# Constant matmuls in TensorE's waits, at the end of a token front and in an attention's lead (Trainium2, one core)

## The reference

```python
h = tok(x)                                  # 36 patches an image: layernorm, 768 -> 256, layernorm, + position
h = concat([cls_tok, h], axis=1)            # 38 tokens an image, width 256
h = h + L0_attn(layernorm(h))               # 16 heads of 16, 4 key/value heads, causal, ternary weights
h = h + L0_ffn(layernorm(h))                # shared expert and one of 8 routed experts
h = h + L1_attn(layernorm(h))               # integer-quantised attention
h = h + L1_ffn(layernorm(h))                # three low-rank-corrected blocks
```

## Time and profile before

| | us |
|---|---|
| median of 3 runs | 531.59 |
| lowest and highest of them | 531.07, 534.79 |
| the profiled execution, its time | 535.75 |
| its span, first to last instruction | 533.9 |
| TensorE busy | 413.0 |
| VectorE busy | 313.8 |
| ScalarE busy | 243.6 |
| GpSimd busy | 154.4 |
| mean granted TensorE clock, as a share of full speed | 0.862 |

### The profile page before, as it was taken

One profiled execution on the slowest core, in us unless ns is written; L12 is line 12 of the kernel. 1 busy time (PEld: TensorE's weight loads), 2 busy tenths in 40 slices (PEclk: granted clock), 3 DMA queues, 4 the chain that ended last, 5 costly groups with the idle time before them and its releaser, 6 DMA issues.

```text
span 533.9 us, 9523 instructions
## 1 busy us (share of the span) xinstructions
PE 413.0 (77%) x3502; PEld 305.2 (57%) x3503; DVE 313.8 (59%) x846; ACT 243.6 (46%) x519; POOL 154.4 (29%) x192
## 2 busy tenths in 40 slices
PE   5788864687999999999889976631894247699997
PEld 4556632565788866666546774210442135589996
DVE  2989877898364212223212137669898987636643
ACT  4345552566554112222122113792397568566651
POOL 3488762899120700000000063017010001213310
PEclk9999986699798999999999997565556556999999
DMA  8941113950033240111110081000000000000002
GB/s 275 401 176 21 21 24 70 425 234 2 1 132 136 92 126 26 54 41 41 39 41 29 26 319 30 1 1 2 2 0 0 1 6 1 1 0 2 1 20 75
DMA packets 19793, 38.64 MB, mean 72 GB/s; under 512 B 2136, under 2 KB 16164, under 8 KB 18340
## 3 DMA queue, kind: packets, MB, share of 16 engines
q1 hardware_dynamic: 18788, 35.41, 19.2%
q0 software_dynamic: 960, 2.62, 1.4%
HBM read 29.77 MB, written 7.01 MB: 69 GB/s over the span
## 4 chain that ended last, share of the span: by engine, by line
PE 56%; DVE 22%; ACT 11%; issue 6%; POOL 3%; DMA 1%; DVEq 0%; SPq 0%; ACTq 0%; POOLq 0%
PE psum L1331 11%; PE psum L1338 6%; PE psum L1363 6%; PE psum L2423 4%; PE psum L1377 4%; PE psum L2456 3%; PE psum L890 2%; PE psum L2462 2%; PE psum L1002 2%; PE psum L1355 1%; ACT experts L1739 1%; PE psum L2440 1%; DVE tile_peak L1767 1%; DVE front L1766 1%; PE psum L641 1%
## 5 line engine op out<-in xcount | busy, mean ns | idle before, releaser
L1331 PE MATMUL psum<-experts,ring 128*128 x136 | 64.3, 596 | 1.9 <-issue 1.2
L1155 DVE TENSOR_TENSOR ring<-ring,psum 128x512 f32<-128x512 f32 x17 | 11.7, 688 | 62.9 <-PE psum L1331 62.9
L1262 POOL DMA_INDIRECT front<-expert_results,slot_of x10 | 9.8, 981 | 125.0 <-DMA expert_results<-ring 122.2
L1338 PE MATMUL psum<-front,shared 128*128 128x256 f32 (+1 forms) x160 | 36.0, 380 | 0.0
L1331 PEld LDWEIGHTS psum<-experts,ring 128*128 128x128 f32 x136 | 23.3, 190 | 19.5 <-issue 19.4
L1338 PEld LDWEIGHTS psum<-front,shared 128*128 128x128 f32 x160 | 30.3, 197 | 3.5
L1363 PE MATMUL psum<-experts,ring 128*128 x136 | 32.1, 379 | 0.0
L1363 PEld LDWEIGHTS psum<-experts,ring 128*128 128x128 f32 x136 | 25.8, 190 | 10.3 <-issue 7.6
L2423 PE MATMUL psum<-experts 128*128 128x256 f32 (+1 forms) x120 | 27.5, 372 | 4.6 <-ACT experts L2486 4.6
L1461 ACT COPY ring<-psum 128x512 f32<-128x512 f32 x17 | 10.0, 586 | 42.4 <-PE psum L1355 42.4
L641 PE MATMUL psum<-experts,ring 128*128 128x256 f32 x108 | 25.1, 382 | 3.5 <-DVE experts L500 1.5
(11 more groups left out here) (364 smaller groups left out, 1081.5 us busy)
## 6 DMA issues: line engine op xcount, KB each, us to landing
experts<-in_experts SPq DMA_DIRECT2D x8, 1536.0 KB, 12.1
experts<-in_x SPq DMA_DIRECT2D x9, 384.0 KB, 8.4
expert_rows<-zeros SPq DMA_DIRECT2D x1, 2176.0 KB, 14.7
ring<-expert_rows SPq DMA_DIRECT2D x17, 128.0 KB, 2.1
shared<-in_shared SPq DMA_DIRECT2D x1, 1536.0 KB, 18.2
experts<-in_ffn_q SPq DMA_DIRECT2D x1, 1536.0 KB
experts<-in_ffn_s SPq DMA_DIRECT2D x1, 1536.0 KB
experts<-in_pos_embed SPq DMA_DIRECT2D x1, 1152.0 KB, 9.3
```

Of the source, the lines that this page charges most:

```text
L1155: nc.vector.tensor_tensor(o, o, up_bank(g), ALU.mult).then_inc(hidden_done.sem, 1)
L1331: mm = nc.tensor.matmul(bank, sl_xT[t % 2][:, k, :], slot_w(t, block, k, F), start=(k == 0), stop=(k == KD - 1))
L1338: mm = nc.tensor.matmul(o[:, b, 0:w], shared_w(block, k, (2 * half + b) * P, P), moe_x(c)[:, k, 0:w], start=(k == 0), stop=(k == KD - 1))
```

## The change

A helper `exercised(bank, times)` issues a number of float32 matmuls whose operands are both constants: the 128x128 identity is the stationary one and 256 columns of the tables (a strictly upper triangular 0/1 matrix and ones) the moving one. Each overwrites the same half bank; nothing reads the result and no semaphore is raised. It is called in two places:

- in the front's loop: at i = 8 (`TOK - 1`) four matmuls into bank 0 between the transposes of the last token tile but one and its projection, at i = 9 two matmuls in the same place, at i = 10 eight matmuls ahead of the last `heads_turned`, and two more after the projection weights are turned;
- in the attention's loop: one into bank 6 ahead of `scores(1)` and of `scores(2)` each, six ahead of `scores(3)`.

These are 24 matmuls, 48 MATMUL records and 48 weight loads. No other engine's program changes, and no wait is added.

```diff
--- before.py
+++ after.py
@@ -624,6 +624,13 @@
                 nc.gpsimd.memset(att_p[u][:, :, SEQ:KEYPAD], 0.0)
             nc.gpsimd.memset(yT[:, :, TOKENS:PADDED], 0.0).then_inc(att_cleared.sem, 1)
 
+        dense = tab[:, WHERE["upper"][0]:WHERE["upper"][0] + 2 * P]
+
+        def exercised(bank, times):
+
+            for _ in range(times):
+                nc.tensor.matmul(psum[:, bank, 0:2 * P], ident, dense, start=True, stop=True)
+
         def front_tensor(pe):
             def patches_turned(t):
                 pe.wait_ge(l_x[t].sem, l_x[t].all)
@@ -728,10 +735,15 @@
                     rows_turned(i)
                     if i + 2 < TOK:
                         patches_turned(i + 2)
+                    if i >= TOK - 1:
+                        exercised(XT, 4 if i == TOK - 1 else 2)
                     projected(i)
+                if i == NT:
+                    exercised(XT, 8)
                 for n in z_items(i - 1):
                     heads_turned(n)
             ternary_proj_turned()
+            exercised(XT, 2)
 
         def front_scalar(act):
             def patches_kept(t):
@@ -904,6 +916,8 @@
             pe.wait_ge(qkT_ready.sem, qkT_ready.done(NT - 1))
             pe.wait_ge(v_zeroed.sem, v_zeroed.done(0))
             for p in range(PAIRS + 4):
+                if 1 <= p <= 3:
+                    exercised(6, 6 if p == 3 else 1)
                 if p < PAIRS:
                     scores(p)
                 if 0 <= p - 3 < PAIRS:
```

## The result

| | before | changed |
|---|---|---|
| median of 20 runs each, us | 533.56 | 530.35 |
| lowest and highest, us | 530.35, 536.22 | 528.30, 536.64 |
| ratio, with its 95% interval | | 0.9948 (0.9930 to 0.9966) |
| profiled execution: time, span, us | 535.75, 533.9 | 528.66, 526.8 |
| mean granted clock of that execution | 0.862 | 0.895 |

What follows compares the result with a forecast made beforehand. Front's end bound by a dependence chain through TensorE at two points, attention by VectorE. Weighted clock cases gave -0.35 us, with 0.2 for the lead about -0.2: from 531.59 to 531.4 us, range 529.3 to 535.5.

Steps and rivals of the forecast that it cites:

- the first rival: Clock holds right through front's end and attention's lead: all of -1.3 us comes, 530.3 us from the median; chance 0.17.
- Four hide and bring the projection back to 1.56 us, 0.7 us: At i = 8, 1.7 us of fill fits the 2.49 us wait; projection takes 1.56 instead of 2.25 us, 0.7 gained.
- Two at i = 9 and eight at i = 10 hide: Front: 0.86 us in a 1.18 us wait, 3.4 us in 5.28 us; about 3.0 us of wait left.
- The last transposes 0.55 or 0.90 us: Front's end: 0.90 us if the clock has fallen by 87.2 us, else 0.55, a gain of 0.35 us.
- the two cost nothing at full clock and 0.9 us at half: After the projection weights: 0.86 us nearly hidden at full clock; at half, 1.7 us in a 0.8 us wait.
- The first scores 0.52 us, 0.3 us gained: Attention's lead: at full clock the first scores take 0.52 instead of 0.81 us, 0.3 us on the path.
- the turns nothing: Attention's lead: the turns of 1.97 us get shorter, but behind a VectorE without a gap, so worth nothing.
- The lead's fill, 0.2 us booked: Ahead of scores(1) to scores(3): hidden at full clock; six at half clock would delay scores(3), partly absorbed by slack; 0.2 us cost.
- The weights of the sum: Clock fallen by 87.2 us, +0.2 us: 0.45; falling from 87.2 to 89, about -0.5: 0.35; holding, -1.3: 0.2.
- The full hold: Clock holds through front's end and lead, -1.3 us; weighted 0.2 within the sum, chance 0.17 as a rival.
- The half-clock fill: Fill in front and lead runs at half clock and becomes the delay: +3.6 us, 535.2 us, tail to 540; chance 0.13.
- Does not do what it says: Clock moves as before; fills hidden except the two after the projection weights, +0.9 us, 532.5 us; chance 0.10.

Runs made afterwards that it cites:

- the attention's part alone: Changed kernel with all fill calls of the front removed, only the eight constant matmuls of the attention's lead left; 0.9995 of the kernel before.
- zeros: Changed kernel with a tile of zeros as moving operand in place of the triangle and the ones, same size; 0.9958 of the kernel before.
- without the two: Changed kernel without the two constant matmuls between the turned projection weights and the first scores; 0.9951 and, measured again, 0.9977 of the kernel before.
- its three sets: Changed kernel against the kernel before, first measurement and two unaltered repeats: 0.9948, 0.9995 and 0.9977.
- fourteen and without the two: Changed kernel with fourteen instead of eight matmuls ahead of the last transposes and none after the turned projection weights; 1.0005 of the kernel before.
- The front's part alone: Changed kernel without the attention's constant matmuls, only the sixteen of the front left; 0.9969 of the kernel before.
- without the eight: Changed kernel without the eight constant matmuls at i = 10 ahead of the last transposes; 1.0001 of the kernel before.

## Why the prediction was right or wrong

The time, 530.35 us, lies in the range, and within 1% of the kernel before, the case with 0.92. The forecast of 0.2 us gained was too low: by the means it is 2.2 us, and 3.2 by the medians of the first set. That 531.4 came within 1.1 us of the result is luck. It started from 531.59 us, the median of three runs, where the median of twenty is 533.56; a start 2.0 us too low and a gain 3.0 us too small nearly cancel. From 533.56 the same sum would have given 533.4, and the first rival 532.3.

- **Four hide and bring the projection back to 1.56 us, 0.7 us.** Right: 12.45 or 12.46 instead of 13.13 and 13.15 us in every profile with the four. It is not owed in every execution, as the attention's part alone shows; I had not thought of that.
- **Two at i = 9 and eight at i = 10 hide; about 3.0 us of wait stay.** Right: 0.50 and 2.98 us left at 1.03 and 3.62 us of fill.
- **The last transposes 0.55 or 0.90 us; the two cost nothing at full clock and 0.9 us at half.** Right in size (0.95). Both states occurred.
- **The first scores 0.52 us, 0.3 us gained; the turns nothing.** Right: 5.65 instead of 5.94 us, and the same rhythm of VectorE.
- **The lead's fill, 0.2 us booked.** Too much; at most 0.1 us, and nothing where the clock held. The single matmul at half clock is 1.15 us where it alternates with the scores, the upper bound, but the slack took it.
- **The weights of the sum.** This is the step that failed. I gave 0.45 to a clock fallen by 87.2 us and 0.2 to one that holds, and argued from the pause of 2.49 us that had lost it before. In the seven profiles with eight constant matmuls ahead of the last transposes, the clock was full there in five (the changed kernel three times, zeros, without the two once) and had fallen in two. The likeliest case was my first rival, -1.3 us, which came out at 1.34 us in its own terms. (The full hold stood both in the sum, with 0.2, and beside it as a rival, with 0.17.) Nor does the pause of 2.49 us always lose the clock: the attention's part alone held it over 2.47 us at the same place. What I left out is that the 3.0 us of rest now stand between dense work on either side; the pause of 2.49 us stood in a stretch of 3.2 us with 0.71 us of work. That this made the difference is argued, not shown: with the same 2.98 us two of the seven lost the clock.
- **The rest.** By the means of its three sets the gain is 2.2 us, by the terms 1.3 in the executions in which all of them are earned. The first set alone, with 1.8 to 3.7 us by its interval, lies above the terms. One candidate is the falls near 133, 144 and 164 us, worth 3.3 us together in the profiles: the change moves those stages by over a microsecond against the instants at which the clock changes, and none of the three profiles of the changed kernel has them. But the attention's part alone and two others without a held clock don't have them either, and fourteen profiles are too few to tell a shifted chance from luck. The mean clocks leave it little room: they make 136 us at half clock before and 116 changed, 20 us less, while the 6.8 and 17.0 us at half clock in the front's end and the lead are 24 us alone. Had the three falls, some 10 us at half clock, gone too in most executions, the difference would be over 30. That stays open, and so does why the version with fourteen and without the two, which earned all of its terms in its profile, was not faster in its runs.
- **Transposes and the clock.** The Trainium skill ("TensorE: Matmul & The Clock Gate", Part 4: PE-mode transpose) says that the full clock doesn't engage for them and that they don't count as busy in the same way. The front's part alone has no constant matmul in the lead, and its clock rose at 104.4 us after scores and two rounds of turns, which made 2.26 of the 3.09 us that TensorE worked in the last 3.2; that agrees with the earlier trace rows and speaks against the page. No kernel was made that tests transposes alone.
- **The rivals.** The half-clock fill (535.2 us) did not happen: the fill itself holds the clock, even with zeros. "Does not do what it says" fell with the first profile.

No version here is shown to beat the changed kernel. Without the two there is a loss less in some executions, by the rows of its second profile; its 24 runs have a mean of 531.2 us against 530.8 for the 42 of the changed kernel.

## What to carry to other kernels

Filling TensorE's waits pays only where a dependence through TensorE is on the path just behind the fill; here that was 1.3 of some 20 us, while of the 17 us at half clock from 85.7 us on only the last transposes and the first scores cost anything, 0.64 us, and the rest, beside a VectorE without gaps, nothing. Price the fill at both clock levels: a fill that fits its wait at full clock and exceeds it at half (the two ahead of the first scores, 0.95 us) loses in some executions what the others gain. And where single executions scatter by several microseconds, compare distances between the same rows over several profiles; here they repeat within 0.02 us at the same clock and tell what 12 runs of the total can't. And before the total of one profile is believed, its mean clock has to be set beside those of the other runs.

## What the runs showed of the hardware that was not expected

- The time of one and the same kernel goes with its granted clock. Over 114 runs of the kernel before, each microsecond at half clock more goes with 0.28 us more time, and from 126 us at half clock (3 runs) to 147 (6 runs) the mean goes from 531.3 to 536.1 us. For 54 runs of the changed kernel and the one with zeros it is 0.19 us. Where the microseconds lie decides their price: the mean clocks, 0.872 before and 0.890 changed, make about 20 us less at half clock for a gain of some 2 us, so most of it was time in which TensorE was not waited for.
- A TensorE without a gap can stay at half clock. In the kernel before it is busy for all of these 18.2 us, where line 2292 alternates with matmuls of 32 rows (PE first, clock third from the right):

```profile
386.30:404.50 18.20, 18.20 (x33) 8.11 (x33) 18.09 (x29) 16.75 (x36) 2.27 (x2) 0.50 0.00 0
```

- Zeros as the moving operand hold the clock like ones (mean 0.892 and 0.890).
- A TensorE matmul of 256 float32 columns at half clock takes 0.85 us from start to start in a run of its own kind (line 1002 near 145 us in the kernel before, and the constant matmuls at 88.8 us in the kernel without the eight) and 1.15 us from start to start where it alternates with matmuls of 32 rows, as beside the scores and at line 2292.
- Amid one pair of the attention TensorE pauses on nothing that the profile shows, in eleven of fourteen profiles and for up to 2.35 us (its row stands with the second profile without the two). The traces point to its own instructions. Count all of TensorE's records in order of time, weight loads and semaphore waits too: in all eleven the pause has exactly 1473 or exactly 1729 of them ahead of it, 256 apart, whatever the program does at that point. It ends 1.2 to 1.5 us after a 16384-byte packet of the kind "instruction" has landed (in the second profile without the two the packet lands at 111.82 us and TensorE goes on at 113.17). In the front's part alone and without the eight, record 1473 stands behind a semaphore wait, and no pause shows. No kernel was made that tests this.
